# Attention and routed-expert kernel: when VectorE copies the transposed probabilities out of PSUM, and five smaller moves

## The chip, the cores and the metric

One core of a Trainium2 chip runs the whole program. The metric is the device time of one execution in microseconds (us), lower is better. Five engines work side by side, each through its own list of instructions in order: PE (TensorE; its weight loads are shown apart as PEld), DVE (VectorE), ACT (ScalarE), POOL (GpSimd) and SP (SyncE, which here issues DMAs). They meet only at semaphores.

## The reference

Sixteen batches of 512 rows with 128 features. For each batch, with `xn` the layer norm of `x`:

```
q, k, v = xn @ Wq + bq, xn @ Wk + bk, xn @ Wv + bv      # 16 heads of 64
att  = softmax(causal(q k^T / 8)) / 8
attn = concat_heads(att v) @ proj
gate = softmax(l2norm(xn Wp^T + bp) @ l2norm(sim) * exp(min(temp, c)))
ffn  = xn W^T + gate_top1 * (xn Wd_e^T) Wu_e^T          # the one expert of four with the largest gate
out  = x + attn + ffn
```

All is float32. The kernel splits float32 operands into a high and a low part ("hi", "lo") and adds three products.

## The kernel before, in words

A batch is 32 **units**, one a step `s`: a pair of heads (8 pairs) times a block of 128 query rows (4 blocks). Unit `s` is block `s % 4` of pair `s // 4`, and has 128 * (s % 4 + 1) key columns, since later keys are masked. In step `s` each engine does its own part of several units, in an order written out by hand in its function `step`:

- PE: `score` writes the scores of unit s, head 0 then head 1 (L1226, L1229 for s % 4 = 0; else L1247 and L1250 for each head). Then `transpose` turns the probabilities of unit s-3, both heads, into `ptp[0]` and `ptp[1]` (L1259). Then a job, if step s has one: k for the next pair (L1130) at s % 4 = 0, v (L1135) at 2, 6, 10, 14, 18, 22, 29, 30, q (L1130) at s % 4 = 3. At s % 4 = 1 come the 32 value matmuls of a pair (L1283), in some steps parts of the output projection (L1295), at 24 the base layer (L1304, L1309).
- DVE: `maximum` (L939) reads the scores of unit s out of PSUM, head 0 then head 1, adds the mask, and writes the row minimum of the negated scores through an accumulator read; `router` does its pieces of the expert choice; `reciprocals` (L927) inverts the sums of unit s-1; `evacuate_pt` (L951) copies head 1 of the turned unit s-3 out of `ptp[1]`; `low_z` (L957) makes the low half of a pair's z; then the low halves of k and q (L825, L829) and the statistics of the layer norm.
- ACT: exponentials of unit s (L688), head 0 of the turned unit s-3 (L699), high halves, v.
- POOL: probabilities times reciprocals (L603), low half of k (L567), a few router and norm operations.

There is one PSUM bank of scores for each head. So PE waits on `sm_ready`, which each maximum raises, before it writes a bank again. For s % 4 = 0 both heads lie in bank 0. Before scores of the steps after it the wait is:

```
wait(pe, sm_ready, c.head(s - 1, 1 if i == 1 else h))      # i = s % 4, for i > 0
```

that is, for unit 4p+1 both maxima of unit 4p must be done before head 0; for units 4p+2 and 4p+3 head h waits for the maximum of head h of the unit before. In turn `evacuate_pt` waits on `t_ready`, which PE raises after the last transpose of head 1, later in the same step than both heads' scores.

Ahead of the first batch PE turns the weights and makes the first q and k. `LATER` are three jobs of the first batch that lie outside the loop: v 0, v 1 (steps 29, 30) and q 1 (step 31). SP loads everything; `projs` (512 KB) is the last of the loads, and k_twice is then filled by small DMAs from k_hi.

Of the kernel before, what the change touches and what calls it, by code (L numbers as in the profile page):

```python
# [40 lines left out]
P = 128  # L41
# [32 lines left out]
LAG_Z = 10  # L74
# [137 lines left out]
def build(nc, x, Wq, bq, Wk, bk, Wv, bv, proj, W, Wp, bp, sim, temp, Wd, Wu, out):  # L212
    with ExitStack() as ctx:
# [187 lines left out]
        def _(sp):  # L401
# [23 lines left out]
            sp.dma_start(projs, proj.rearrange("(c p) e -> p c e", p=P)).then_inc(proj_loaded, 16)  # L425

# [70 lines left out]
        def _(pool):  # L497
# [80 lines left out]
            for h in range(2):  # L578
# [4 lines left out]
            nc.gpsimd.tensor_tensor(gated_t[:], token_heads[:, 0:S], token_heads[:, S:2 * S], ALU.add)\  # L583
                .then_inc(heads_marked, 1)
            pool.wait_ge(heads_marked, 4)
            pool.wait_ge(proj_loaded, 16)
            nc.gpsimd.tensor_copy(proj_hi[:], projs).then_inc(proj_split, 1)
            pool.wait_ge(proj_split, 1)
            nc.gpsimd.tensor_tensor(proj_lo[:], projs, proj_hi[:].bitcast(F32), ALU.subtract).then_inc(proj_split, 1)

            def sim_root():
                pool.wait_ge(simsq_ready, 1)
                nc.gpsimd.tensor_tensor(sim_norm[:, 1, :], sim_norm[:, 0, :], power[:, 1, 0:NEXP], ALU.pow)\
                    .then_inc(simnorm_ready, 1)
                pool.wait_ge(simnorm_ready, 1)

# [8 lines left out]
            def batch(b, last):  # L605
                c = Counts(pool, b)
                for s in range(UNITS):
# [19 lines left out]
                    if b == 0 and s == 0:  # L627
                        sim_root()
                    if s in JOBS and JOBS[s][0] == "k" and not (last and s in AHEAD):
                        pad_low_keys(c, s)  # L630
                    if s == STEP_RSTD and not last:
# [13 lines left out]
        def _(act):  # L645
# [79 lines left out]
            weights(4)  # L725

# [26 lines left out]
            def batch(b, first, last):  # L753
                c = Counts(act, b)
                for s in range(UNITS):
                    step(c, s, first, last)
                    if first and s == 0:
                        for js in LATER:
                            job(setup, js)
                        weights(5)  # L760
                    if first and s == 1:
                        gate_factor()
# [23 lines left out]
        def _(dve):  # L786
# [100 lines left out]
            def similarities():  # L887
                dve.wait_ge(sim_loaded, 32)
                nc.vector.tensor_scalar(temp_c[:], temp_b[:], CLAMP_MAX, None, ALU.min).then_inc(temp_ready, 1)
                link(nc.vector.tensor_tensor(sim_sq[:], sim_b[:], sim_b[:], ALU.mult))  # L890
                nc.vector.tensor_reduce(sim_norm[:, 0, :], sim_sq[:].rearrange("p a b -> p b a"), AX_X, ALU.add)\
                    .then_inc(simsq_ready, 1)
# [36 lines left out]
            def maximum(c, s):  # L929
                cols = width(s)  # L930
                for h in range(2):
                    bank, first_col = place(s, h)
                    scored, turned = c.fixed(c.head(s, 1 if s % NBLK == 0 else h)), c.fixed(c.head(s - NROT, h))

                    dve.wait_ge(consts_ready, 3)
                    dve.wait_ge(s_ready, scored)

                    wait(dve, t_ready, turned)
                    nc.vector.tensor_tensor_reduce(  # L939
                        out=prob[:, s % NROT, h, 0:cols], in0=scores[bank][:, first_col:first_col + cols], in1=mask[:, S - cols:S],  # L940
                        scale=-INV_SCALE, scalar=HUGE, op0=ALU.add, op1=ALU.min,
                        accum_out=nmax[:, s % NROT, h:h + 1]).then_inc(sm_ready, 1)
# [23 lines left out]
            def router(c, t):  # L966


                def prior(n):
                    dve.wait_ge(r_chain, c.at(R_CHAIN, n))  # L970

                def over_experts(m):
                    return m.unsqueeze(2).to_broadcast([P, NBLK, NEXP])

                t -= R_FIRST
                logits, shifted, exps, weights, chosen, ranked, first, routed = (lg[:, n, :, :] for n in range(1, 9))
                if t == 0:
# [4 lines left out]
                if t == 6:  # L982

                    dve.wait_ge(unorm_root, c.at(1, 1))
                    prior(1)
                    nc.vector.tensor_tensor(logits, lg[:, 0, :, :], over_experts(unorm[:, 2, :]), ALU.mult)\
                        .then_inc(r_chain, 1)
                if t == 6:
                    prior(2)
                    nc.vector.tensor_reduce(row[:, 0, :], logits, AX_X, ALU.max).then_inc(r_chain, 1)  # L990
                if t == 7:
                    prior(3)
                    nc.vector.tensor_tensor(shifted, logits, over_experts(row[:, 0, :]), ALU.subtract)\
                        .then_inc(lg_ready, 1)
                if t == 13:
# [3 lines left out]
                if t == 13:  # L999
                    prior(4)  # L1000
                    nc.vector.reciprocal(row[:, 2, :], row[:, 1, :]).then_inc(r_chain, 1)
                if t == 14:
                    prior(5)
                    nc.vector.tensor_tensor(weights, exps, over_experts(row[:, 2, :]), ALU.mult).then_inc(r_chain, 1)
                if t == 14:
                    prior(6)
                    nc.vector.tensor_reduce(row[:, 3, :], weights, AX_X, ALU.max).then_inc(r_chain, 1)
                if t == 15:
                    prior(7)
                    nc.vector.tensor_tensor(chosen, weights, over_experts(row[:, 3, :]), ALU.is_ge)\  # L1010
                        .then_inc(r_chain, 1)
                if t == 15:
                    prior(8)
# [410 lines left out]
```

## Time and profile before

| | us |
|---|---|
| three runs | 1374.68, 1376.75, 1377.0; median 1376.75 |
| the profiled execution, its own time | 1376.77 |
| its span, first to last instruction | 1375.0 |
| PE busy | 1350.0 (98%) |
| DVE busy | 1106.6 (80%) |
| ACT busy | 1077.1 (78%) |
| POOL busy | 971.9 (71%) |

The span is the program as the profile shows it; the 1.8 us between span and time lie around it. A matmul's row shows its start and how long it is under way; matmuls overlap, so what one costs is the distance from its start to the next one's start. The same holds for VectorE, whose rows overlap their successors by some 0.1 us.

### The profile page before, as it was taken

The numbers are of one execution on the slowest core, as the hardware profiler recorded it, in microseconds if no ns is written. First come the engines' busy times: TensorE is split into PE (matmuls) and PEld (weight loads), VectorE is DVE, ScalarE is ACT, GpSimd is POOL, SyncE is SP. The second block draws the span as 40 slices with busy tenths as digits, with TensorE's granted clock in tenths as the row PEclk, the third lists the DMA queues.
The fourth block names the chain that finished last, engine by engine and source line by source line (L and its number), as shares of the span: only waits on it lengthen the run. The fifth ranks groups of instructions, "written<-read, shape, count | busy, mean of one in ns | idle before, by whom it ended". The sixth has DMA issues, their size and how long they took to land.

```text
span 1375.0 us, 34724 instructions
## 1 busy us (share of the span) xinstructions
PE 1350.0 (98%) x10925; PEld 1140.4 (83%) x10925; DVE 1106.6 (80%) x4015; ACT 1077.1 (78%) x3161; POOL 971.9 (71%) x1421
## 2 busy tenths in 40 slices
PE   6999999999999999999999999999999999999998
PEld 4788888888888888888888888888888888888886
DVE  6877878788787887879788787887878878787784
ACT  4787877878777787787778878777887887878784
POOL 5777766777767777767777677776676776677664
PEclk9999999999999999999999999999999999999999
DMA  5444444444445445444544544444454444445441
GB/s 128 108 112 105 116 120 97 116 110 115 108 105 131 98 104 125 112 109 103 117 112 105 123 103 110 112 116 113 95 121 118 101 116 113 119 94 118 114 101 47
DMA packets 112690, 150.87 MB, mean 110 GB/s; under 512 B 18239, under 2 KB 47230, under 8 KB 112510
## 3 DMA queue, kind: packets, MB, share of 16 engines
q1 hardware_dynamic: 111646, 148.36, 45.6%
q8 instruction: 91, 1.49, 0.5%
q14 instruction: 89, 0.73, 0.2%
q10 hardware_dynamic: 864, 0.29, 0.1%
HBM read 10.69 MB, written 4.19 MB: 11 GB/s over the span
## 4 chain that ended last, share of the span: by engine, by line
PE 90%; DVE 5%; issue 1%; SPq 0%; DMA 0%; ACT 0%; DVEq 0%
PE zp L1283 22%; PE ptp L1259 20%; PE jobp L1130 12%; PE scores L1247 11%; PE scores L1250 9%; PE outp L1295 6%; PE jobp L1135 5%; DVE prob L939 2%; PE scores L1229 1%; DVE pt L951 1%; PE scores L1226 1%; PE jobp L1145 1%; PE outp L1304 1%; DVE z_lo L957 1%; PE jobp L1150 1%
## 5 line engine op out<-in xcount | busy, mean ns | idle before, releaser
L603 POOL TENSOR_TENSOR prob<-prob,rden 128x128 f32<-128x128 f32 (+3 forms) x1024 | 713.4, 724 | 347.2 <-DVE rden L927 345.1
L939 DVE CUSTOM_DVE_ANT_0 prob<-scores,mask 128x128 f32<-128x128 f32 (+3 forms) x1024 | 461.8, 488 | 220.8 <-issue 203.4
L688 ACT ACTIVATE prob<-prob,nmax 128x128 f32<-128x128 f32 (+3 forms) x1024 | 567.1, 559 | 38.9 <-DVE nmax L939 38.8
L1259 PE MATMUL ptp<-ident,prob 128*128 128x128 f32 x2560 | 375.7, 275 | 6.4 <-DVE pt L951 5.6
L1259 PEld LDWEIGHTS ptp<-ident,prob 128*128 128x128 f32 x2560 | 293.4, 141 | 44.8 <-issue 16.0
L1283 PE MATMUL zp<-pt,v_sb 128*64 128x64 f32 (+3 forms) x4096 | 307.7, 303 | 0.2 <-ACT pt L699 0.2
L699 ACT ACTIVATE pt<-ptp 128x128 f32<-128x128 f32 (+3 forms) x512 | 220.6, 431 | 108.2 <-PE ptp L1259 106.5
L1247 PE MATMUL scores<-k_twice,q_parts 128*128 128x256 f32 (+2 forms) x768 | 268.2, 357 | 0.3 <-DVE nmax L939 0.3
L1283 PEld LDWEIGHTS zp<-pt,v_sb 128*64 128x64 f32 x4096 | 221.3, 137 | 51.7 <-issue 19.5
L1250 PE MATMUL scores<-k_low,q_parts 128*128 128x256 f32 (+2 forms) x768 | 253.7, 338 | 0.0
L951 DVE COPY pt<-ptp 128x128 f32<-128x128 f32 (+3 forms) x512 | 243.2, 475 | 2.1 <-PE ptp L1259 1.3
L688 ACT ACTIVATION_READ_ACCUMULATOR prob<-prob,nmax 128x1 f32 x1024 | 199.9, 195 | 0.0
L1247 PEld LDWEIGHTS scores<-k_twice,q_parts 128*128 128x128 f32 x768 | 144.0, 188 | 62.9 <-issue 42.7
L567 POOL CAST k_low<-k_lo 64x512 fp32r<-64x512 f32 x256 | 156.9, 613 | 35.0 <-DVE k_lo L825 21.2
L677 ACT ACTIVATE z_hi<-zp 128x512 fp32r<-128x512 f32 x128 | 76.7, 599 | 131.8 <-PE zp L1283 131.8
L1250 PEld LDWEIGHTS scores<-k_low,q_parts 128*128 128x128 f32 x768 | 144.7, 188 | 15.2
L829 DVE SCALAR_TENSOR_TENSOR q_lo<-jobp,bqk,q_hi 128x512 fp32r<-128x512 f32 x128 | 95.6, 747 | 7.2 <-ACT q_hi L669 2.0
L825 DVE SCALAR_TENSOR_TENSOR k_lo<-jobp,bqk,k_hi 128x512 fp32r<-128x512 f32 x128 | 95.1, 743 | 1.8 <-ACT k_hi L666 1.7
L957 DVE TENSOR_TENSOR z_lo<-zp,z_hi 128x512 fp32r<-128x512 f32 x128 | 87.1, 680 | 2.4 <-ACT z_hi L677 2.4
L666 ACT ACTIVATE k_hi<-jobp,bqk 128x512 fp32r<-128x512 f32 x128 | 87.0, 680 | 0.2 <-PE jobp L1194 0.2
L669 ACT ACTIVATE q_hi<-jobp,bqk 128x512 fp32r<-128x512 f32 x128 | 86.1, 672 | 0.8 <-PE jobp L1184 0.7
L939 DVE DVE_READ_ACCUMULATOR2_ANT nmax<- 128x1 f32 x1024 | 85.1, 83 | 0.2
(183 smaller groups left out, 1841.7 us busy)
## 6 DMA issues: line engine op xcount, KB each, us to landing
k_twice<-k_hi SPq DMA_DIRECT2D x508, 128.0 KB, 2.3
q_parts<-q_lo SPq DMA_DIRECT2D x256, 128.0 KB, 2.4
q_parts<-q_hi SPq DMA_DIRECT2D x254, 128.0 KB, 2.3
xin<-in_L_attn_x_dram SPq DMA_DIRECT2D x16, 256.0 KB, 3.7
xres<-in_L_attn_x_dram SPq DMA_DIRECT2D x16, 256.0 KB, 3.1
out_dram<-osb SPq DMA_DIRECT2D x15, 256.0 KB, 2.6
pt<-in_L_attn_Wq_dram SPq DMA_DIRECT2D x1, 512.0 KB, 4.5
pt<-in_L_attn_Wk_dram SPq DMA_DIRECT2D x1, 512.0 KB, 6.2
```

The lines of the kernel that those rows point to most:

```text
L567: nc.gpsimd.tensor_copy(k_low[own(h), h, n % 2, :], k_lo[own(h), :].bitcast(F32))\
L603: nc.gpsimd.tensor_tensor(part, part, scale, ALU.mult).then_inc(pn_ready, 1)
L688: nc.scalar.activation(part, part, ACT.Exp, bias=nmax[:, s % NROT, h:h + 1], scale=-1.0, accum_out=den[:, s % NROT, h:h + 1]).then_inc(p_r ...
L699: nc.scalar.activation(pt[:, p % 2, 0, 0:i + 1, P * i:P * i + P], src, ACT.Copy)\
L939: nc.vector.tensor_tensor_reduce(out=prob[:, s % NROT, h, 0:cols], in0=scores[bank][:, first_col:first_col + cols], in1=mask[:, S - cols:S ...
L951: nc.vector.tensor_copy(pt[:, p % 2, 1, 0:i + 1, P * i:P * i + P], src).then_inc(pt_ready[1], 1)
L957: nc.vector.tensor_tensor(low, both, high.bitcast(F32), ALU.subtract).then_inc(z_ready, 1)
L1130: done = nc.tensor.matmul(dst[:], a[w][:, cols], m[:], start=a is w_hi and m is high, stop=a is w_lo)
L1247: nc.tensor.matmul(scores[h][:, 0:width(s)], q_parts[:, h, p % 2, queries], k_twice[:, h, p % 2, 0:width(s)], start=True, stop=False)
L1250: nc.tensor.matmul(scores[h][:, 0:width(s)], q_parts[:, h, p % 2, queries], k_low[:, h, p % 2, 0:width(s)], start=False, stop=True).then_i ...
L1259: done = nc.tensor.transpose(ptp[h][:, P * j:P * j + P], prob[:, s % NROT, h, P * j:P * j + P], ident[:])
L1283: done = nc.tensor.matmul(zp[DH * odd:DH * odd + DH, z0 + P // 2 * j:z0 + S // 2], v_sb[:, j, col:col + DH], seen, start=j == NBLK - 1, st ...
```

## The change

1. In DVE's `step`, `maximum` is called for one head at a time, and `reciprocals` and `evacuate_pt` stand between the two. 2. `low_z` follows a step later (11 steps behind instead of 10). 3. The router chain moves: its parts stand in steps 5, 6, 7, 9, 10 and 13 instead of 6 to 15, in groups of two to six operations; the aggregates of the norm move from step 13 to 17. 4. PE makes v 0 and v 1 ahead of the first scores and only q 1 after them; ACT evacuates them there. 5. SP issues the load of `projs` after the first q and k moves have landed; POOL splits `projs` after its second unit instead of ahead of the first. 6. In the first steps of batch 0 two weight parts, the similarities and the up-weights change places on DVE, ACT and POOL.

The core of the diff:

```diff
-LAG_Z = 10
+LAG_Z, LAG_LOW_Z = 10, 11
...
-STEPS_STATS, STEP_AGGR, STEP_VAR = (5, 9), 13, 17
+STEPS_STATS, STEP_AGGR, STEP_VAR = (5, 9), 17, 17
...
-STEP_PRODUCTS, STEP_UNORM, STEP_EXPERTS = 3, 6, 11
+STEP_PRODUCTS, STEP_UNORM, STEP_EXPERTS = 3, 4, 7
 R_CHAIN = 14
-R_FIRST = 12
+STEP_SUMS, STEP_LOGITS, STEP_WEIGHTS, STEP_FIRST, STEP_PARTS = 5, 6, 9, 10, 13
...
-            sp.dma_start(projs, proj.rearrange("(c p) e -> p c e", p=P)).then_inc(proj_loaded, 16)
...
+            sp.wait_ge(qk_moved[0], setup.moved(NPAIR))
+            sp.dma_start(projs, proj.rearrange("(c p) e -> p c e", p=P)).then_inc(proj_loaded, 16)
...
             def step(c, s, first=False, last=False, tail=False):
-                if not tail:
-                    maximum(c, s)
-                    router(c, 2 * s)
-                unit = due(s, 1, 1, first, tail)
-                if unit is not None:
-                    reciprocals(c, unit)
-                unit = due(s, LAG_T, 1, first, tail)
-                if unit is not None:
-                    evacuate_pt(c, unit)
-                p = due(s, LAG_Z, NBLK, first, tail)
+                def follow():
+                    unit = due(s, 1, 1, first, tail)
+                    if unit is not None:
+                        reciprocals(c, unit)
+                    unit = due(s, LAG_T, 1, first, tail)
+                    if unit is not None:
+                        evacuate_pt(c, unit)
+
+                maximum(c, s, 0)
+                follow()
+                maximum(c, s, 1)
+                router_early(c, s)
+                p = due(s, LAG_LOW_Z, NBLK, first, tail)
                 if p is not None:
                     low_z(c, p)
                 if s == STEP_FINAL and not first:
                     final(c)
-                if tail:
-                    return
+                router_late(c, s)
...
@@ PE, ahead of the first step, and in it
+            pe.wait_ge(w_lo_ready, 3)
+            for s in LATER[:2]:
+                job(setup, s)
             pe.wait_ge(small_ready, 3)
...
                 if first and s == 0:
-                    later()
+                    job(setup, LATER[2])
```

`router_early` holds the groups of steps 5, 6 and 10, `router_late` those of 9 and 13; the operations are those of `router`. On POOL the split of `projs` (L587, L589) moves into `projection_parts`, called after step 1 of batch 0.

In steady state the lists of PE, ACT and SP are the same as before. On DVE, the end of a step with s % 4 = 2 and the start of the next, in batch 0 (L939 is the maximum, L951 the copy of the turned unit, L927 the reciprocal, L957 z's low half; in the changed file L943, L955, L932, L961). Before:

```order
L939 ISA prob,nmax<-scores,mask 128x384
L939 ISA nmax 128x1
L939 ISA prob,nmax<-scores,mask 128x384
L939 ISA nmax 128x1
L927 RECIPROCAL rden<-den 128x2
L951 COPY pt<-ptp 128x4x128
L957 TENSOR_TENSOR z_lo<-zp,z_hi 128x8x64
```

and in the changed kernel:

```order
L943 ISA prob,nmax<-scores,mask 128x384
L943 ISA nmax 128x1
L932 RECIPROCAL rden<-den 128x2
L955 COPY pt<-ptp 128x4x128
L943 ISA prob,nmax<-scores,mask 128x384
L943 ISA nmax 128x1
```

The copy of four blocks now stands ahead of the second maximum, and z's low half is gone from this step. The step with s % 4 = 0, before:

```order
L939 ISA prob,nmax<-scores,mask 128x128
L939 ISA nmax 128x1
L939 ISA prob,nmax<-scores,mask 128x128
L939 ISA nmax 128x1
L927 RECIPROCAL rden<-den 128x2
L951 COPY pt<-ptp 128x2x128
L829 SCALAR_TENSOR_TENSOR q_lo<-jobp,bqk,q_hi 128x512
```

and in the changed kernel:

```order
L943 ISA prob,nmax<-scores,mask 128x128
L943 ISA nmax 128x1
L932 RECIPROCAL rden<-den 128x2
L955 COPY pt<-ptp 128x2x128
L943 ISA prob,nmax<-scores,mask 128x128
L943 ISA nmax 128x1
L835 SCALAR_TENSOR_TENSOR q_lo<-jobp,bqk,q_hi 128x512
```

Here too the copy (two blocks) stands ahead of the second maximum. On PE, from the last weight part to q 1 ahead of and in the first step; before (L1226 and L1229 are the first scores, L1135 is v, L1130 q):

```order
L1163 MATMUL ptp<-ident,pt 128x128 x8
L1226 MATMUL scores<-k_low,q_hi 128x256
L1229 MATMUL scores<-k_twice,q_parts 128x128 x2
L1135 MATMUL jobp<-w_hi,xt_hi 128x512
L1135 MATMUL jobp<-w_lo,xt_hi 128x512
L1135 MATMUL jobp<-w_hi,xt_lo 128x512
L1135 MATMUL jobp<-w_hi,xt_hi 128x512
L1135 MATMUL jobp<-w_lo,xt_hi 128x512
L1135 MATMUL jobp<-w_hi,xt_lo 128x512
L1130 MATMUL jobp<-xq_hi,w_hi 128x512
```

and in the changed kernel (L1218 and L1221 the scores, L1129 v, L1124 q):

```order
L1157 MATMUL ptp<-ident,pt 128x128 x8
L1129 MATMUL jobp<-w_hi,xt_hi 128x512
L1129 MATMUL jobp<-w_lo,xt_hi 128x512
L1129 MATMUL jobp<-w_hi,xt_lo 128x512
L1129 MATMUL jobp<-w_hi,xt_hi 128x512
L1129 MATMUL jobp<-w_lo,xt_hi 128x512
L1129 MATMUL jobp<-w_hi,xt_lo 128x512
L1218 MATMUL scores<-k_low,q_hi 128x256
L1221 MATMUL scores<-k_twice,q_parts 128x128 x2
L1124 MATMUL jobp<-xq_hi,w_hi 128x512
```

The six matmuls of v 0 and v 1 now stand ahead of the first scores.

## Rows read from the trace of the kernel before

**Rows 1.** The page, part 1: busy time of each engine, share, instructions.
```profile
PE 1350.0 (98%) x10925; PEld 1140.4 (83%) x10925; DVE 1106.6 (80%) x4015; ACT 1077.1 (78%) x3161; POOL 971.9 (71%) x1421
```

**Rows 2.** Waits of PE: who, until whom; us in all, times, longest.
```profile
PE ptp L1259 <- DVE pt L951: 5.6, 17, 0.8
PE scores L1247 <- DVE nmax L939: 0.3, 1, 0.3
```

**Rows 3.** Timeline of PE, steps 2 and 3 of batch 7: start, us, what.
```profile
613.56 1.03 PE L1259 MATMUL ptp<-ident,prob 128*128 128x128 f32 x8
...
615.59 0.39 PE L1247 MATMUL scores<-k_twice,q_parts 128*128 128x512 f32 x1
```

**Rows 4.** Timeline of DVE over the same stretch.
```profile
613.50 0.56 DVE L939 CUSTOM_DVE_ANT_0 prob<-scores,mask 128x384 f32<-128x384 f32 x1 [2.16 <-issue]
...
613.98 0.55 DVE L939 CUSTOM_DVE_ANT_0 prob<-scores,mask 128x384 f32<-128x384 f32 x1
...
614.63 0.69 DVE L951 COPY pt<-ptp 128x512 f32<-128x512 f32 x1
615.24 0.68 DVE L957 TENSOR_TENSOR z_lo<-zp,z_hi 128x512 fp32r<-128x512 f32 x1
```

**Rows 5.** Timeline of PE in batch 0, a score matmul that waited for DVE.
```profile
34.90 0.38 PE L1247 MATMUL scores<-k_twice,q_parts 128*128 128x256 f32 x1 [0.27 <-DVE nmax L939]
35.12 0.28 PE L1250 MATMUL scores<-k_low,q_parts 128*128 128x256 f32 x1
```

**Rows 6.** Timeline of DVE, the accumulator read which that matmul waited for.
```profile
34.76 0.08 DVE L939 DVE_READ_ACCUMULATOR2_ANT nmax<- 128x1 f32 x1
```

**Rows 7.** Timeline of PE, steps 4 and 5 of batch 7.
```profile
617.97 0.62 PE L1259 MATMUL ptp<-ident,prob 128*128 128x128 f32 x4
...
618.90 0.39 PE L1130 MATMUL jobp<-xt_hi,w_lo 128*128 128x512 f32 x1
619.13 0.28 PE L1247 MATMUL scores<-k_twice,q_parts 128*128 128x256 f32 x1
619.24 0.28 PE L1250 MATMUL scores<-k_low,q_parts 128*128 128x256 f32 x1
```

**Rows 8.** Timeline of PEld, the weight load of the matmul at 619.13.
```profile
618.90 0.19 PEld L1247 LDWEIGHTS scores<-k_twice,q_parts 128*128 128x128 f32 x1
```

**Rows 9.** Timeline of DVE over the same stretch.
```profile
618.27 0.29 DVE L939 CUSTOM_DVE_ANT_0 prob<-scores,mask 128x128 f32<-128x128 f32 x1 [0.81 <-issue]
...
618.49 0.29 DVE L939 CUSTOM_DVE_ANT_0 prob<-scores,mask 128x128 f32<-128x128 f32 x1
...
618.78 0.41 DVE L951 COPY pt<-ptp 128x256 f32<-128x256 f32 x1
619.10 0.74 DVE L829 SCALAR_TENSOR_TENSOR q_lo<-jobp,bqk,q_hi 128x512 fp32r<-128x512 f32 x1
```

**Rows 10.** Timeline of PE, steps 26 and 27 of batch 7.
```profile
676.28 1.03 PE L1259 MATMUL ptp<-ident,prob 128*128 128x128 f32 x8
...
677.67 0.41 PE L1247 MATMUL scores<-k_twice,q_parts 128*128 128x512 f32 x1
```

**Rows 11.** Timeline of DVE, step 8 of batch 7: end of a maximum, next reciprocal.
```profile
628.64 0.08 DVE L939 DVE_READ_ACCUMULATOR2_ANT nmax<- 128x1 f32 x1
628.73 0.17 DVE L927 RECIPROCAL rden<-den 128x2 f32<-128x2 f32 x1
```

**Rows 12.** Timeline of PE, the first score matmul of the program.
```profile
19.00 0.55 PE L1226 MATMUL scores<-k_low,q_hi 128*128 128x256 f32 x1 [4.53 <-DMA k_twice<-k_hi]
```

**Rows 13.** Timeline of DVE, low half of the third weight part, before it.
```profile
15.37 0.69 DVE L869 TENSOR_TENSOR w_lo<-zp,w_hi 128x512 fp32r<-128x512 f32 x1 [0.43 <-ACT w_hi L649]
```

**Rows 14.** Windows: busy by engine, then PE's granted clock, DMA share, GB/s.
```profile
19.00:22.30 3.30, 3.30 (x9) 2.73 (x10) 2.24 (x9) 1.48 (x5) 2.38 (x1) 0.50 0.00 0
...
26.70:28.30 1.60, 0.30 (x2) 0.00 (x0) 0.76 (x2) 1.60 (x6) 0.99 (x2) 1.00 0.66 166
28.30:31.90 3.60, 3.56 (x24) 3.21 (x25) 3.46 (x13) 2.06 (x8) 2.46 (x4) 1.00 0.73 195
```

More of the change, by code:

```diff
@@ L595, in sim_root, with projection_parts @@
                 pool.wait_ge(simnorm_ready, 1)
+            sim_root()
+            nc.gpsimd.tensor_tensor(gated_t[:], token_heads[:, 0:S], token_heads[:, S:2 * S], ALU.add)\
+                .then_inc(heads_marked, 1)
+            pool.wait_ge(heads_marked, 4)
+            def projection_parts():
+                pool.wait_ge(proj_loaded, 16)
+                nc.gpsimd.tensor_copy(proj_hi[:], projs).then_inc(proj_split, 1)
+                pool.wait_ge(proj_split, 1)
+                nc.gpsimd.tensor_tensor(proj_lo[:], projs, proj_hi[:].bitcast(F32), ALU.subtract)\
+                    .then_inc(proj_split, 1)
             def normalise(c, s):
@@ L725, in _ @@
             weights(4)
+            for js in LATER[:2]:
+                job(setup, js)
             def gate_factor():
@@ L757, in batch @@
                     if first and s == 0:
-                        for js in LATER:
-                            job(setup, js)
+                        job(setup, LATER[2])
+                        gate_factor()
+                    if first and s == 1:
                         weights(5)
-                    if first and s == 1:
-                        gate_factor()
             batch(0, True, False)
@@ L927, in reciprocals, with maximum @@
                 nc.vector.reciprocal(rden[:, s % NROT, :], den[:, s % NROT, :]).then_inc(r_ready, 1)
-            def maximum(c, s):
+            def maximum(c, s, h):
                 cols = width(s)
[L931 to L942, printed above, removed]
+                bank, first_col = place(s, h)
+                scored, turned = c.fixed(c.head(s, 1 if s % NBLK == 0 else h)), c.fixed(c.head(s - NROT, h))
+                dve.wait_ge(consts_ready, 3)
+                dve.wait_ge(s_ready, scored)
+                wait(dve, t_ready, turned)
+                nc.vector.tensor_tensor_reduce(
+                    out=prob[:, s % NROT, h, 0:cols], in0=scores[bank][:, first_col:first_col + cols],
+                    in1=mask[:, S - cols:S], scale=-INV_SCALE, scalar=HUGE, op0=ALU.add, op1=ALU.min,
+                    accum_out=nmax[:, s % NROT, h:h + 1]).then_inc(sm_ready, 1)
             def evacuate_pt(c, s):
@@ L964, in final, with over_experts, router_early @@
                                         xres[:].rearrange("p n e -> p (n e)"), ALU.add).then_inc(final_ready, 1)
[L966 to L977, printed above, removed]
+            def over_experts(m):
+                return m.unsqueeze(2).to_broadcast([P, NBLK, NEXP])
+            logits, shifted, exps, shares, chosen, ranked, top, routed = (lg[:, n, :, :] for n in range(1, 9))
+            def router_early(c, s):
+                if s == STEP_SUMS:
                     dve.wait_ge(products_ready, c.at(1, 1))
@@ L1005, in router @@
[L1005 to L1010, printed above, removed]
+                    dve.wait_ge(r_chain, c.at(R_CHAIN, 5))
+                    nc.vector.tensor_tensor(shares, exps, over_experts(row[:, 2, :]), ALU.mult).then_inc(r_chain, 1)
@@ L1068, in step @@
                     variances(c)
-                router(c, 2 * s + 1)
             def batch(b, first, last):
@@ L1076, in batch @@
                         weights(3)
+                        job(before, LATER[2])
+                    if first and s == 1:
                         weights(4)
-                        similarities()
-                        for js in LATER:
-                            job(before, js)
                         experts_up()
-                    if first and s == 1:
                         weights(5)
@@ L1203, in _ @@
             weights(4)
+            pe.wait_ge(w_lo_ready, 3)
+            for s in LATER[:2]:
+                job(setup, s)
             pe.wait_ge(small_ready, 3)
-            def later():
-                pe.wait_ge(w_lo_ready, 3)
-                for s in LATER:
-                    job(setup, s)
             def value_bias():
@@ L1326, in step @@
                 if first and s == 0:
-                    later()
+                    job(setup, LATER[2])
                 unit = due(s, LAG_T, 1, first, tail)
```

75 lines of the change are left out of this document (30 added, 45 removed).

## The prediction

> **What bounds the kernel now.** I read the page first, then the waits of PE, then the timelines of PE and DVE side by side through one pair of heads in the middle of the run. PE is busy 98% of the span, the next engine, DVE, 80% [rows 1]. PE's waits for DVE are small: 5.6 us in 17 waits for the copy L951, about one a batch, and 0.3 us for a maximum [rows 2]. So PE runs its list almost without a hole, and the time is the length of that list. After the first steps the change leaves PE's list as it is; it can only take holes out of it or put holes into it. What it moves is DVE, and DVE's idle time (2.16 us ahead of one maximum, 0.81 us ahead of another [rows 4, 9]) says that DVE has time to spare on average. The question is whether DVE is late at the moments when PE asks.
>
> PE asks twice in a pair, and closely: ahead of head 1 of unit 4p+3 it needs the second maximum of unit 4p+2, and ahead of head 0 of unit 4p+1 the second maximum of unit 4p. Before, the second maximum followed the first at once. Now the copy L951 stands between, and the copy waits for PE's own transposes of the same step. This makes a closed loop inside a step: PE's last transpose, DVE's copy, DVE's second maximum, PE's next scores. Its length does not depend on how idle DVE is otherwise.
>
> **The loop from step 4p+2 to 4p+3.** PE's eight transposes start at 613.56 and end at 613.56 + 1.03 = 614.59; head 1 of the next scores starts at 615.59 [rows 3]. PE gives DVE 1.00 us. DVE needs: 0.04 until the copy starts (614.63, just behind the transposes; its first maximum was done long before), 0.61 for the copy of four blocks (614.63 to 615.24), 0.48 for the maximum of 384 columns (613.50 to 613.98) [rows 4], 0.08 for its accumulator read, which ends at 34.84, and 0.06 until PE goes on at 34.90 [rows 5, 6]. Sum 1.27, so PE starts 0.27 late. There is a second part. A matmul that had to wait starts with its weight load, and the next one comes 0.22 behind it (34.90 to 35.12) [rows 5]; where nothing waits the distance is 0.11 (619.13 to 619.24) [rows 7]. That adds 0.11. Hole: **0.38 us**, at 7 of the 8 pairs of a batch.
>
> A rule bears on the 0.11. The load of the matmul at 619.13 starts at 618.90, together with the matmul ahead of it [rows 7, 8], so a load in time costs nothing. The Trainium skill says (TensorE: Matmul & The Clock Gate, section Measured speedup vs the span model) that weight loads overlap running matmuls only where they use other row groups; both of these use all 128 rows, so by it no load would be hidden now, a late one would add nothing, and the sum below would be 26 us less. The trace does not agree with it.
>
> **The loop at step 26** has no v job between the transposes and the next scores: 676.28 + 1.03 = 677.31, and head 1 starts at 677.67 [rows 10], 0.36 after. DVE's 1.27 leaves 0.91, with the load 1.02 us, once a batch.
>
> **The loop from step 4p to 4p+1.** The four transposes end at 617.97 + 0.62 = 618.59, PE's next scores start at 619.13 [rows 7]: 0.54. DVE: 0.04, 0.32 for the copy of two blocks (618.78 to 619.10), 0.22 for the maximum of 128 columns (618.27 to 618.49) [rows 9], then 0.08 and 0.06 as above, 0.72. Late by 0.18, with the load **0.29 us**. It falls on 7 pairs; in step 24 four wide matmuls (base and experts) lie between and cover it.
>
> The other two transitions cost nothing: between 4p+1 and 4p+2 PE has 32 value matmuls, and head 0 of unit 4p+4 needs only the first maximum of 4p+3.
>
> A batch: 7 x 0.38 + 7 x 0.29 + 1.02 = 5.71 us, 16 batches: **+91.4 us**. What is queued behind the waiting copy on DVE (second maximum, low halves of k and q, z) comes later by about half a microsecond and is taken up by DVE's idle time of 0.81 and 2.16 us in the same pair [rows 4, 9]. ACT's exponential of head 1 waits with it; ACT, busy 78% of the span [rows 1], has the idle time for that. But the reciprocal, which needs that exponential, now also stands ahead of the second maximum. Where it waited in the trace it was 0.09 us (628.64 to 628.73) [rows 11]. I take nothing for it, and 0.09 at each of the 15 places as the upper end (+22 us).
>
> **What goes away.** The router's chain leaves the steps in which PE waited for L951, and the copy comes ahead of the second maximum: the 17 waits of 5.6 us [rows 2] go, with their 17 late loads of 0.11: **-7.5 us**. The router's operations themselves are the same and are put at nothing: the largest group stands in step 9, ahead of the idle 2.16 us; without that cover they would delay the first maximum of step 10, which PE needs only before step 11.
>
> **z's low half a step later** is put at nothing. It moves into the step ahead of the 0.81 us idle [rows 9], and PE overwrites z only two steps on. Without that cover it would push the next first maximum and with it the loop at 4p.
>
> **The start.** PE stood idle 4.53 us until k_twice had landed, and started the first scores at 19.00 [rows 12]; so it was free at 14.47. The 512 KB of `projs` were issued just ahead of the transfers that it waited for. Now `projs` comes after them, and PE has v 0 and v 1 to do, which need the low half that DVE ends at 15.37 + 0.69 = 16.06 [rows 13]. The hole shrinks to 1.59: **-2.9 us**. The ends are nothing (POOL now splits `projs` between two units, where PE or DVE may wait for it) and -4.5 (the whole hole). The exchanges of small operations in steps 0 to 3 lie within these ends.
>
> Sum against the profiled execution, 1376.8 us by its own time, which is also the median of the runs: 1376.8 + 91.4 - 7.5 - 2.9 = **1457.8 us**, 5.9% slower.
>
> **The rivals.**
> - *The loop is shorter than PE's own way.* If copy and maximum overlapped or PE's 1.00 and 0.54 us were longer, no hole would open; it decides at 0.27 and 0.18 us. Then only the savings are left: 1376.8 - 7.5 - 2.9 = 1366.4, faster. For it: DVE has 20% to spare. Against it: the distances are the same in every pair that I looked at, and DVE goes in order. 8%.
> - *Only the longer loop holds* (the one at 4p is hidden because copy and maximum are short): without 16 x 7 x 0.29 = 32.5 us, 1425. For it: it is late by 0.18 only. Against: the terms are measured to hundredths. 5%.
> - *The late load is free*, the page's rule above: without 16 x 15 x 0.11 = 26.4, 1431. Against it: the two distances [rows 5, 7]. 5%.
> - *The clock falls.* After the idle 4.53 us PE ran 3.3 us at a granted clock of 0.50, the lower of its two levels (1.2 and 2.4 GHz), but through a hole of 1.3 us (0.30 busy in 1.60) and after it at 1.00 [rows 12, 14]. If the 1.0 us hole of step 26 made it fall for as long, a batch would lose 3.3 / 2 = 1.65 more, 16 times 26: 1484. The Trainium skill (the same page, section A second HAM failure mode: psum-queue depth-cycling) tells of a kernel whose short idle times between groups of matmuls made the clock swing. No stretch after the start shows that here. 5%.
> - *The change does not do what it says*: the order of DVE's list shows that it does; no chance of its own.
>
> **How the numbers follow.** Chances: forecast 77%, the rivals 8, 5, 5 and 5%. A measurement can tell about 0.2% from no change. Faster is the first rival, 8%; within 0.2% would need holes that just cancel the savings, 1%; slower the rest, 91%. The range: downwards, the late loads free (-26.4) and the hole at step 26 half as long (-8), 1423; upwards, every reciprocal late by 0.09 (+22) and nothing saved at the start (+3), 1482. It takes in the second and third rival and leaves out the first and the clock.
>
> **What would show it.** In the profile after: waits of PE for DVE's nmax ahead of the score matmuls, some 15 a batch, 240 in all, of 0.2 to 1.0 us; PE's busy share near 93%; idle DVE just ahead of the copies of four blocks; no wait of PE for L951; the first scores by 18.8 or earlier; the clock at 1.00 throughout. It is wrong if those waits are few, if they sit in front of other matmuls, or if a batch is not near 89 us instead of 83.8.

## The result and the profile after

The changed kernel takes **1445.86 us** (median of 5 runs, 1445.18 to 1446.13) against 1377.0 us before: ratio 1.0503, 95% interval 1.0487 to 1.0518. It is 69 us slower; the prediction was 1457.8 us, range 1423 to 1482. Its profiled execution has a span of 1443.7 us and a granted clock of 1.000.

The page of the changed kernel, part 1, and groups of part 5 (busy us, mean ns | idle just before, what ended most of it):

```profile
PE 1399.1 (97%) x10925; PEld 1124.3 (78%) x10925; DVE 1144.1 (79%) x4015; ACT 1103.3 (76%) x3161; POOL 969.7 (67%) x1421
...
L943 DVE CUSTOM_DVE_ANT_0 prob<-scores,mask 128x128 f32<-128x128 f32 (+3 forms) x1024 | 495.7, 485 | 155.1 <-issue 136.1
L1251 PE MATMUL ptp<-ident,prob 128*128 128x128 f32 x2560 | 365.9, 274 | 0.0
L955 DVE COPY pt<-ptp 128x128 f32<-128x128 f32 (+3 forms) x512 | 250.2, 489 | 98.9 <-PE ptp L1251 89.4
```

VectorE now stands idle 98.9 us ahead of the copies, waiting for PE's transposes; the transposes no longer wait for the copy (5.6 us before, [rows 2]). PE, which bounds the kernel, still reads 97% busy [rows 1 had 98%], although its list became 5% longer. The waits, of all engines, show where the time is:

```profile
PEld scores L1239 <- DVE nmax L943: 138.2, 256, 2.4
...
DVE pt L955 <- PE ptp L1251: 89.4, 236, 1.3
...
PE scores L1239 <- DVE nmax L943: 14.4, 29, 2.0
```

Under PE itself there are 29 waits of 14.4 us; the other ones stand under PEld, the weight load, which is the instruction that waits. The load's engine has idle time anyway, so 138.2 us is no cost, and PE's row understates it, since the modelled end of one matmul lies over most of a short hole. What a hole costs has to be read from starts. Here is the loop from step 4p+2 to 4p+3 in batch 7, the stretch of [rows 3, 4], PE first:

```profile
641.21 1.04 PE L1251 MATMUL ptp<-ident,prob 128*128 128x128 f32 x8
...
643.50 0.50 PE L1239 MATMUL scores<-k_twice,q_parts 128*128 128x512 f32 x1
643.83 0.40 PE L1242 MATMUL scores<-k_low,q_parts 128*128 128x512 f32 x1
```

and VectorE:

```profile
641.15 0.56 DVE L943 CUSTOM_DVE_ANT_0 prob<-scores,mask 128x384 f32<-128x384 f32 x1 [1.86 <-issue]
...
642.28 0.69 DVE L955 COPY pt<-ptp 128x512 f32<-128x512 f32 x1 [0.48 <-PE ptp L1251]
642.89 0.55 DVE L943 CUSTOM_DVE_ANT_0 prob<-scores,mask 128x384 f32<-128x384 f32 x1
643.36 0.08 DVE L943 DVE_READ_ACCUMULATOR2_ANT nmax<- 128x1 f32 x1
```

The transposes end at 642.25. The copy starts 0.03 later, the second maximum 0.61 after that, its read ends at 643.44, and PE goes on at 643.50: 1.25 us after the transposes, where it took 1.00 before [rows 3]. This is the loop of the prediction link by link.

To price every place, the starts of PE's matmuls in two kernels were set side by side, position by position in a batch (PE's list is the same in all these kernels after the first batch), and the differences averaged over 11 batches. "Excess" below means that. From router matmul to router matmul a batch takes 88.27 us (median), against 83.75 before.

### The profile page after: what moved, and what is told of

Its sections match the earlier page's. It is cut to its first block and busy times, and to the rows that moved or that the text cites. A ratio compares the mean times of both kernels' runs of the same rounds, so it can differ in the third digit from the quotient of the medians.

```text
span 1443.7 us, 34725 instructions
## 1 busy us (share of the span) xinstructions
PE 1399.1 (97%) x10925; PEld 1124.3 (78%) x10925; DVE 1144.1 (79%) x4015; ACT 1103.3 (76%) x3161; POOL 969.7 (67%) x1421
## 5 line engine op out<-in xcount | busy, mean ns | idle before, releaser
L943 DVE CUSTOM_DVE_ANT_0 prob<-scores,mask 128x128 f32<-128x128 f32 (+3 forms) x1024 | 495.7, 485 | 155.1 <-issue 136.1
L1251 PE MATMUL ptp<-ident,prob 128*128 128x128 f32 x2560 | 365.9, 274 | 0.0
L955 DVE COPY pt<-ptp 128x128 f32<-128x128 f32 (+3 forms) x512 | 250.2, 489 | 98.9 <-PE ptp L1251 89.4
L1239 PE MATMUL scores<-k_twice,q_parts 128*128 128x256 f32 (+2 forms) x768 | 292.1, 388 | 30.7 <-DVE nmax L943 14.4
L1239 PEld LDWEIGHTS scores<-k_twice,q_parts 128*128 128x128 f32 x768 | 143.9, 187 | 185.9 <-DVE nmax L943 138.2
L961 DVE TENSOR_TENSOR z_lo<-zp,z_hi 128x512 fp32r<-128x512 f32 x128 | 87.6, 685 | 2.5 <-ACT z_hi L682 2.5
L932 DVE RECIPROCAL rden<-den 128x2 f32<-128x2 f32 x512 | 83.0, 162 | 5.4 <-ACT prob L693 3.7
```

Source lines behind the costliest of these rows:

```text
L943: nc.vector.tensor_tensor_reduce(out=prob[:, s % NROT, h, 0:cols], in0=scores[bank][:, first_col:first_col + cols], in1=mask[:, S - cols:S ...
L955: nc.vector.tensor_copy(pt[:, p % 2, 1, 0:i + 1, P * i:P * i + P], src).then_inc(pt_ready[1], 1)
L1239: nc.tensor.matmul(scores[h][:, 0:width(s)], q_parts[:, h, p % 2, queries], k_twice[:, h, p % 2, 0:width(s)], start=True, stop=False)
L1251: done = nc.tensor.transpose(ptp[h][:, P * j:P * j + P], prob[:, s % NROT, h, P * j:P * j + P], ident[:])
```

## The experiments

The runs of the kernel before that stood beside these have medians of 1375.5 to 1376.4 us. All kernels are edits of the changed one, but for the second and the ninth, which start from the kernel before.

### 1. Copy behind both maxima again

```diff
                 maximum(c, s, 0)
-                follow()
                 maximum(c, s, 1)
+                follow()
```

> The changed kernel with one thing undone: both maxima first, then reciprocals and copy, as before; z's low half, the router's steps and the start stay changed. Theory (the copy ahead of the second maximum makes the holes): the holes of about 5.6 us a batch go, 16 x 5.6 = 90 us, and what is left is the start, -3.7 us, and up to -1.0 us a batch; 1357 to 1373 us, so faster than before; PE's waits for nmax nearly none. Rival 1 (z's low half or the router's groups make DVE late): stays at 1430 to 1446 us. Rival 2 (the copy and the moves each do harm only together): also far under 1446, told apart by the next run.

**1359.28 us, ratio to the kernel before 0.9876 (0.9861 to 0.9891): faster than both.** One edit of two lines takes away 86.6 us. A batch takes 82.88 us. The excess of the changed kernel over this one is 5.39 us a batch (x16 = 86.2) and stands in the places named by the prediction and hardly anywhere else:

| place | of each, predicted | excess: late + late load |
|---|---|---|
| 4p+2 to 4p+3, 7 a batch | 0.27 + 0.11 | 0.26 + 0.105 |
| 4p to 4p+1, 7 a batch | 0.18 + 0.11 | 0.20 + 0.10 |
| step 26 to 27, once | 0.91 + 0.11 | 0.34 ahead of head 0, 0.57 + 0.09 at head 1 |
| transposes at two later places | nothing | -0.10, -0.08 |

### 2. The copy between, and nothing else of the change

In the kernel before, reciprocals and copy stand between the maxima; router, z's low half and the start are those of before.

```diff
-                    maximum(c, s)
-                    router(c, 2 * s)
+                maximum(c, s, 0)
...
                     evacuate_pt(c, unit)
+                maximum(c, s, 1)
+                router(c, 2 * s)
```

> The kernel before with one thing changed: reciprocals and copy between the two maxima; router, z's low half and the start as before. Theory: 1377 + 16 x (5.6 - 0.47) = 1459 us, 1445 to 1470, with PE's waits for nmax in the same three places of a pair (scores of units 4p+1 head 0, 4p+3 head 1, and 4p+3 of the seventh pair about 1.0 us). Rival 2 (harm only together with the other moves): under 1400 us.

**1470.51 us** (ratio 1.0687, 1.0669 to 1.0704), just over the upper end. The copy alone makes the loss, but with the router and z's low half in their old places it costs 94.2 us instead of 86.6. Two of the holes at 4p are wider: 0.79 us ahead of unit 9 and 1.04 us ahead of unit 17, against 0.20 elsewhere. VectorE ahead of the second one:

```profile
690.35 0.34 DVE L1032 CAST gated_parts<-gated 128x256 fp32r<-128x256 f32 x1
690.73 0.80 DVE L1036 TENSOR_TENSOR gated_parts<-gated,gated_parts 128x128 fp32r<-128x128 f32 x1
691.45 0.28 DVE L938 CUSTOM_DVE_ANT_0 prob<-scores,mask 128x128 f32<-128x128 f32 x1
...
691.73 0.40 DVE L950 COPY pt<-ptp 128x256 f32<-128x256 f32 x1
692.05 0.27 DVE L938 CUSTOM_DVE_ANT_0 prob<-scores,mask 128x128 f32<-128x128 f32 x1
```

Two router operations of step 15 push the first maximum of step 16 to 691.45, and the whole chain of the step with it. With the router in its new steps no such hole stands anywhere. Ahead of unit 9 it is the reciprocal that is late (VectorE, ScalarE, VectorE, PE):

```profile
665.25 0.68 DVE L980 TENSOR_REDUCE lg<-uprod 128x16 f32<-128x512 f32 x1
```

```profile
667.17 0.73 ACT L688 ACTIVATE prob<-prob,nmax 128x512 f32<-128x512 f32 x1 [0.63 <-DVE nmax L938]
```

```profile
668.88 0.17 DVE L927 RECIPROCAL rden<-den 128x2 f32<-128x2 f32 x1 [0.60 <-ACT prob L688]
```

```profile
669.63 0.39 PE L1246 MATMUL scores<-k_twice,q_parts 128*128 128x256 f32 x1 [0.63 <-DVE nmax L938]
```

Router sums and z's low half at the end of step 6 push the maxima of unit 7, ScalarE waits 0.63 us for the first of them, and the reciprocal of unit 7, which stands between the maxima of step 8, waits 0.60 us for them, with the copy and the second maximum behind it. It does so in each of the 11 batches, and in the changed kernel in none. No run took this alone.

### 3 and 4. One loop at a time

The steps are 1, 2, 3 in the first kernel and 0, 1, 3 in the second.

```diff
+                between = s % NBLK in (1, 2, 3)
                 maximum(c, s, 0)
-                follow()
+                if between:
+                    follow()
                 maximum(c, s, 1)
+                if not between:
+                    follow()
```

> The changed kernel with copy and reciprocals between the maxima only in steps with s % 4 = 1, 2, 3; in steps with s % 4 = 0 they stand behind both maxima. Theory: only the loop from 4p+2 to 4p+3 is left, 7 x (0.263 + 0.104) + 1.015 = 3.58 us a batch: 57 us over the kernel with the copy behind both maxima everywhere, about 1415 to 1430. If the two loops share their cost (DVE late from one into the other), more than 57.

> The changed kernel with copy and reciprocals between the maxima only in steps with s % 4 = 0, 1, 3. Theory: only the loop from 4p to 4p+1 is left, 7 x (0.19 + 0.10) = 2.03 us a batch: 32 us over the kernel with the copy behind both maxima everywhere, about 1390 to 1405. The rival of the prediction that only the longer loop holds: no more than 5 us over it. The excess of this run and of the one with s % 4 = 1, 2, 3, added, should give the whole distance between the changed kernel and the one with the copy behind both maxima, to within 5 us.

**1412.09 us and 1396.74 us**, 52.8 and 37.5 over experiment 1. The sum is 90.3, the whole distance 86.6: within the 5 us. Each kernel has the seven holes of its own loop at the same size as in the changed kernel and none of the other's. So the two loops hold independently, and the rival with the longer loop alone is out: without what the odd steps cost (4.5 us, the next experiment) the 4p loop comes to 32.9 us, 32.5 predicted. One thing does not fit the prediction: 0.34 us ahead of head 0 of unit 27 stand in both kernels, and so does the gain of 0.10 at the transposes of step 24. Counted twice in the sum, they are 16 x 0.24 = 3.8 us of it, which is about its distance from 86.6.

### 5. Copy between in steps 4p+1 and 4p+3 only

```diff
+                between = s % NBLK in (1, 3)
```

> The changed kernel with copy and reciprocals between the maxima only in steps with s % 4 = 1 and 3. Theory of the prediction: these transitions cost nothing, 1359 us. But in the run with s % 4 = 0, 1 and 3 a hole of 0.34 us was left ahead of head 0 of unit 27: if the copy of step 25 makes it, it stands here too, 16 x 0.34 = 5.4 us, 1365; if the copy of step 24 does, 1359.

**1363.81 us**, 4.5 over experiment 1. The 0.33 us ahead of unit 27 are here too, so the copy in an odd step makes them. The chain goes through ScalarE, as the trace of the changed kernel shows behind step 25:

```profile
704.18 0.51 ACT L693 ACTIVATE prob<-prob,nmax 128x256 f32<-128x256 f32 x1 [0.28 <-DVE nmax L943]
...
704.69 0.58 ACT L667 ACTIVATE xt<-jobp 128x512 f32<-128x512 f32 x1
705.16 0.59 ACT L668 ACTIVATE xq_hi<-jobp 128x512 fp32r<-128x512 f32 x1
```

and VectorE after that, PE last:

```profile
705.85 0.91 DVE L823 TENSOR_TENSOR xq_lo<-xt,xq_hi 128x512 fp32r<-128x512 f32 x1 [1.04 <-ACT xq_hi L668]
706.68 0.68 DVE L839 TENSOR_TENSOR xt_lo<-xt,xt_hi 128x512 fp32r<-128x512 f32 x1
707.28 0.55 DVE L943 CUSTOM_DVE_ANT_0 prob<-scores,mask 128x384 f32<-128x384 f32 x1
...
707.76 0.15 DVE L932 RECIPROCAL rden<-den 128x2 f32<-128x2 f32 x1
707.84 0.67 DVE L955 COPY pt<-ptp 128x512 f32<-128x512 f32 x1
708.42 0.54 DVE L943 CUSTOM_DVE_ANT_0 prob<-scores,mask 128x384 f32<-128x384 f32 x1
```

```profile
706.71 1.04 PE L1251 MATMUL ptp<-ident,prob 128*128 128x128 f32 x8
707.89 0.50 PE L1239 MATMUL scores<-k_twice,q_parts 128*128 128x512 f32 x1
...
709.03 0.50 PE L1239 MATMUL scores<-k_twice,q_parts 128*128 128x512 f32 x1 [0.40 <-DVE nmax L943]
```

The late second maximum of unit 25 delays ScalarE's exponential of head 1, behind it the three evacuations of the turned norm (L667 to L669), and these VectorE's two halves (L823, L839), which stand ahead of the first maximum of unit 26. PE waits for both heads of unit 27.

### 6. Only the reciprocals between

```diff
                 maximum(c, s, 0)
+                inverse()
                 maximum(c, s, 1)
+                copy()
```

> The changed kernel with only the reciprocals between the maxima and the copy behind both. Theory (the copy's wait for the same step's transposes makes the holes): as with both behind, 1359 us, 1355 to 1364, hole by hole. Rival (the reciprocal, which waits for ACT's exponential of head 1, holds the second maximum back): 0.09 us at 15 places a batch, up to 22 us more, 1381.

**1359.11 us**, the same as experiment 1. With the router in its new steps the reciprocal's price is nil.

### 7. Other work between the maxima

```diff
                 maximum(c, s, 0)
+                p = due(s, LAG_Z, NBLK, first, tail)
+                if p is not None:
+                    low_z(c, p)
                 maximum(c, s, 1)
```

with reciprocals and copy behind both maxima.

> The changed kernel with z's low half between the two maxima of the steps with s % 4 = 2 (10 steps behind, as in the kernel before), reciprocals and copy behind both maxima. So VectorE does a comparable piece of work between the maxima, but one that waits for nothing of this step's PE. Theory: no closed loop, no holes, 1359 us, 1355 to 1366. Rival (any work between the maxima makes PE late): a hole of the order of 0.2 to 0.4 us in 7 pairs and more at step 26, 25 to 60 us more, 1385 to 1420.

**1374.35 us**, between the two expectations. VectorE in step 4p+2 of batch 7:

```profile
610.94 0.56 DVE L943 CUSTOM_DVE_ANT_0 prob<-scores,mask 128x384 f32<-128x384 f32 x1 [2.16 <-issue]
...
611.42 0.69 DVE L961 TENSOR_TENSOR z_lo<-zp,z_hi 128x512 fp32r<-128x512 f32 x1
612.03 0.55 DVE L943 CUSTOM_DVE_ANT_0 prob<-scores,mask 128x384 f32<-128x384 f32 x1
```

From the start of what stands between to the second maximum it takes 0.61 us here as with the copy (642.28 to 642.89), but nothing waits: the maximum starts at 612.03, just as the transposes end (611.00 + 1.03), and the seven holes are gone. What is left is 0.50 + 0.09 us at step 26, where no v job gives PE anything to do, and 0.27 us at the transposes of steps 8 and 9. So in the seven pairs it is the wait for the same step's transposes that costs; at step 26 0.6 us of work that waits for nothing costs 0.50 us all the same. I had not expected the latter.

### 8. The heads of the copies exchanged

```diff
-                dve.wait_ge(t_ready, c.head(s, 1))
+                dve.wait_ge(t_ready, c.head(s, 0))
...
-                src = ptp[1][:, 0:width(s)].rearrange("p (j q) -> p j q", q=P)
+                src = ptp[0][:, 0:width(s)].rearrange("p (j q) -> p j q", q=P)
```

and the reverse on ScalarE.

> The changed kernel with the heads of the copies exchanged: VectorE copies head 0 of the turned unit, ScalarE head 1. Reciprocals and copy stay between the maxima; but head 0's transposes end about 0.5 us (4 of 8) or 0.3 us (2 of 4) ahead of head 1's, so VectorE is released earlier by that. Theory: the holes at 4p+2 (late by 0.27) and 4p (late by 0.18) go; at step 26 0.91 - 0.5 and the late load, some 0.5 us, is left: 1359 + 16 x 0.5 = 1367, 1357 to 1385. Rival (what counts is the work between the maxima, not its wait): holes as in the changed kernel, 1430 to 1446. ScalarE's copy comes later by as much and may hold back the next transposes; that would show as waits of PE for ACT's pt.

**1400.42 us**: half right. The seven holes at 4p+2 are gone, by the earlier release alone. Those at 4p shrink only from 0.20 to 0.15 + 0.10 at five of seven places and to 0.10 + 0.11 ahead of unit 29; ahead of unit 9 the hole grows to 0.39 + 0.10, which was not followed. Step 26 keeps 0.07 + 0.57 + 0.09. VectorE at 4p in this kernel, where the transposes end at 626.96:

```profile
626.63 0.29 DVE L943 CUSTOM_DVE_ANT_0 prob<-scores,mask 128x128 f32<-128x128 f32 x1 [0.22 <-issue]
...
626.88 0.17 DVE L932 RECIPROCAL rden<-den 128x2 f32<-128x2 f32 x1
626.96 0.40 DVE L955 COPY pt<-ptp 128x256 f32<-128x256 f32 x1
627.28 0.28 DVE L943 CUSTOM_DVE_ANT_0 prob<-scores,mask 128x128 f32<-128x128 f32 x1
```

The copy could start when head 0's transposes are done, but VectorE reaches it only now: first maximum, read and reciprocal take until 626.96. At 4p two chains end within 0.1 us of each other, the wait for the transposes and VectorE's own, and taking one away leaves the other.

### 9 and 10. Where the gain of experiment 1 comes from

The start alone (parts 4 to 6 of the change), in the kernel before; PE's share of it:

```diff
+            pe.wait_ge(w_lo_ready, 3)
+            for s in LATER[:2]:
+                job(setup, s)
...
-                    later()
+                    job(setup, LATER[2])
```

Then experiment 1 with z's low half 10 steps behind:

```diff
-LAG_Z, LAG_LOW_Z = 10, 11
+LAG_Z, LAG_LOW_Z = 10, 10
```

> The kernel before with only the start changed (the values made ahead of the first scores, the load of projs after the first q and k moves, the small exchanges in the first steps); VectorE's order, router and z's low half as before. By the traces the first router matmul comes 3.7 us earlier in the changed kernel (24.74 to 21.04): 1376 - 3.7 = 1372.3 us, 1371 to 1374, and the batches after the first as before. The prediction's term is -2.9 with ends 0 and -4.5. Rival: the split of projs on POOL or the late loads give it back in the first batch, no change.

> The changed kernel with both maxima first and z's low half 10 steps behind again; only the router's steps and the start stay changed. The prediction puts the move of z's low half at nothing: then 1359 us, as with z's low half 11 steps behind, and the 0.86 us a batch that this kernel gains on the one before are the router's. Rival: three of the four gains (0.07 to 0.10 us each, 0.28 a batch) are those of z's low half: 1359 + 16 x 0.28 = 1363.5.

**1374.08 us** (ratio 0.9986, 0.9977 to 0.9995) and **1368.45 us** (0.9946, 0.9934 to 0.9959). The start gives 1.8 us by the medians. In the profiled executions the first router matmul comes 3.8 us earlier, but the first batch takes 0.6 us more and the later ones some 0.6 in all. In the first batch of the changed kernel, the likely reason:

```profile
26.57 1.10 POOL L597 CAST proj_hi<-pt 128x1024 fp32r<-128x1024 f32 x1
27.76 2.38 POOL L599 TENSOR_TENSOR proj_lo<-pt,proj_hi 128x1024 fp32r<-128x1024 f32 x1
...
30.18 0.29 DVE L923 CAST wut<-outp 96x128 fp32r<-96x128 f32 x1 [0.94 <-POOL proj_lo L599]
...
32.17 0.39 PE L1239 MATMUL scores<-k_twice,q_parts 128*128 128x256 f32 x1 [1.97 <-DVE nmax L943]
```

POOL's split of `projs` holds VectorE until 30.14, and PE then stands 1.97 us for a maximum. No run took this alone.

From the start alone to the second of these kernels it is 5.6 us, the router's and aggregates' part: the wait for L951 at step 16 is gone, 0.46 us a batch with its load. And z's low half one step later is worth **9.2 us** (1368.45 to 1359.28), more than the rival had said. With z's low half back, four places among the transposes (steps 8, 9, 13 and 29) lose 0.07 to 0.11 us each, 0.39 of 0.52 us a batch. The places of steps 9 and 29 are late in the kernel before too, those of 8 and 13 only with the router in its new steps: the split between router and z's low half is that of this order of the moves. VectorE from the end of step 6 into step 7:

```profile
620.38 0.68 DVE L961 TENSOR_TENSOR z_lo<-zp,z_hi 128x512 fp32r<-128x512 f32 x1
620.98 0.68 DVE L943 CUSTOM_DVE_ANT_0 prob<-scores,mask 128x512 f32<-128x512 f32 x1
...
621.58 0.68 DVE L943 CUSTOM_DVE_ANT_0 prob<-scores,mask 128x512 f32<-128x512 f32 x1
...
622.19 0.16 DVE L932 RECIPROCAL rden<-den 128x2 f32<-128x2 f32 x1
622.27 0.27 DVE L955 COPY pt<-ptp 128x128 f32<-128x128 f32 x1
```

and PE:

```profile
622.36 0.73 PE L1251 MATMUL ptp<-ident,prob 128*128 128x128 f32 x4
```

z's low half stands ahead of both maxima, so the copy ends at 622.54, after PE has begun the next transposes (622.36); the four take 0.73 us where they take 0.62 in experiment 1. At the transposes of step 9 it is POOL's normalisation that is late, behind the late reciprocal; the other two places were not followed.

### 11. The odd steps but step 25

```diff
+                between = s % NBLK in (1, 3) and s != STEP_BASE + 1
```

> The changed kernel with copy and reciprocals between the maxima only in steps with s % 4 = 1 and 3, but not in step 25. In the run with s % 4 = 1 and 3 the only hole was 0.33 us ahead of head 0 of unit 27, and one late weight load of 0.10 was gone. If step 25 makes that hole: 1359.2 - 16 x 0.10 = 1357.6 us, the fastest of the runs. If another odd step makes it, 1363 again.

**1359.15 us.** The hole ahead of unit 27 is gone, so step 25 was its source, and the gain of 0.10 us at the transposes of step 24 is kept; a batch takes 82.76 us, 0.12 less than in experiment 1. The first batch takes 1.8 us more (82.97 against 81.20; why is open), and the total is no better. Experiments 1, 6 and 11 are the best kernels here, and not told apart.

### 12. Only the copy between

```diff
                 maximum(c, s, 0)
-                follow()
+                unit = due(s, LAG_T, 1, first, tail)
+                if unit is not None:
+                    evacuate_pt(c, unit)
                 maximum(c, s, 1)
+                unit = due(s, 1, 1, first, tail)
+                if unit is not None:
+                    reciprocals(c, unit)
```

> The changed kernel with only the copy between the maxima and the reciprocals behind both. Theory: the copy's wait carries the holes; the reciprocal overlaps its neighbours and is 0.08 us of VectorE's way where nothing else waits (in steps with s % 4 = 0 and in step 26, where in the changed kernel the copy starts straight behind it), nothing where the copy waits for the transposes: 0 to 8 x 0.08 us a batch less, 1435 to 1446 us. Rival, the upper end of the prediction: each reciprocal 0.09 late at 15 places, 22 us less, 1424.

**1446.33 us**, the changed kernel's time; excess 5.44 us a batch over experiment 1, in the same places (ahead of unit 27 0.52 + 0.51 instead of 0.34 + 0.57). The copy alone carries the loss.

## Why the prediction was right

- **The two loops** held, in mechanism and size: seven times 0.37 (0.38 predicted) and seven times 0.30 (0.29). Together with step 26 and the two gains of 0.10 and 0.08 the copy's place costs 86.6 us by experiment 1, 91.4 predicted. For 4p+2 the reason was the given one (experiments 7 and 8). For 4p it was half of it: VectorE's own chain of maximum, reciprocal and copy ends as late as the transposes.
- **Step 26**: 1.00 us, 1.02 predicted. Head 1 starts 1.28 us after the transposes (707.75 to 709.03), the predicted 1.27, but there is a second way to it: 0.34 us of the hole stand ahead of head 0 and come from step 25. "The other two transitions cost nothing" failed there, and so did "has the idle time for that": the maximum of unit 25 delays ScalarE, and with it the first maximum of unit 26, which the prediction, going by the other pairs, took to be "done long before". No run has the copy between in step 26 and not in step 25, so what would be left without the 0.34 is open, and that the size came out so well is in part luck.
- **The late weight load** costs 0.09 to 0.11 us at every place, which makes up 1.5 us a batch. That it is the load is read from the trace and not tested: a load in time starts 0.22 ahead of its matmul (642.54, 642.76), a late one together with it (643.50). The rival that called it free would have 16 x 15 x 0.10 = 24 us less. The Trainium skill has the line behind that rival (TensorE: Matmul & The Clock Gate, section The mechanism; the prediction names the section that follows): weight loads overlap running matmuls only when they use other row groups. The trace does not agree with that line, since the load at 642.54 runs under matmuls that use all 128 rows, as it does. The same section also lets a load into the background weight buffer run ahead; no run here shows whether this is one.
- **The waits for L951**: -7.5 predicted, -5.6 measured with the router's new places (0.46 a batch saved, some of it lost by 0.06 and 0.11 at two transposes).
- **z's low half** was the term that failed: put at nothing, it is worth -9.2 us. I asked only whether it delays the next maximum, and did not see that the copy and the reciprocal behind it come late for PE's next transposes, by some 0.1 us at a time. PE's waits in the profile do not show that: with z's low half back they have one wait for the copy, 0.8 us in the whole run.
- **The start**: -2.9 predicted, -1.8 measured. The first scores start at 17.80 instead of 19.00, behind a hole of 1.29 us (1.59 predicted). The 4.53 us were those of one execution: in experiment 2, which has the start of the kernel before, the hole is 3.31 and the first scores start at 18.39. And the prediction did not count the stretch at a granted clock of 0.50, the lower level [rows 14]. The profiled execution of the changed kernel has none at the start (1.00 from 13 to 40 us), but it depends on the execution: five executions of the kernel before with a mean granted clock of 1.000 took 1375.1 us on average, four of the start alone 1374.2. So of the 1.8 us some 0.9 are left where no such stretch stands in either. Against the start stands the first batch.
- **The reciprocal**, the upper end of +22 us, is nothing in the changed kernel (experiments 6 and 12). With the router in its old steps it does hold the copy back, at one place of a batch (experiment 2, unit 9).
- **The clock** stayed at 1.000 with 256 waits of weight loads on record, and in none of the fourteen profiles did it fall between 39 us and the last 4: the rival of the falling clock is out.

The misses, measured less predicted: holes -4.8, z's low half -9.2, router +1.9, start +1.1, in sum -11.0 of the 11.9 us between forecast and result; the other 0.9 lie in the starting point (1376.8 in the forecast, 1375.9 beside experiment 9). The four terms are the steps of one way from the kernel before to the changed one (1375.9, 1374.1, 1368.5, 1359.3, 1445.9), so that they add up says nothing for any one of them. In another order they come out otherwise: with the other moves still to come the copy's place costs 94.2 us (experiment 2). Of the signs named ahead, one was wrong: PE's busy share is 97%, not 93%, for the reason given with the waits.

## What to carry to other kernels

When an instruction that waits for engine A is put ahead of one that A waits for, write down the closed loop with its times and compare it with A's own time between the two points; idle time of the other engine, here 20%, does not shorten it. Behind each moved instruction, price also the small lateness of what the bound engine reads next: 0.1 us at four places a batch was 6 of the 9 us that z's low half was worth. What stands inside the loop is free only as long as its own inputs come in time: the reciprocal cost nothing in the changed kernel and held the copy 0.60 us in experiment 2. And where an engine runs short overlapping instructions, price holes by distances between starts, not by idle time or busy share.

## What the runs showed of the hardware

The granted clock does not follow from one hole of PE alone (windows: start to end, length, busy PE, PEld, DVE, ACT, POOL, clock, DMA share, GB/s). In experiment 1 PE stood for 2.27 us up to 32.13, and the clock then fell to 0.50, the lower of its two levels:

```profile
33.50:36.50 3.00, 3.00 (x14) 2.77 (x13) 3.00 (x10) 1.64 (x6) 2.92 (x5) 0.50 0.66 154
```

In the changed kernel the hole of 1.97 us at the same place left it at 1.00:

```profile
34.00:37.00 3.00, 2.43 (x14) 1.83 (x15) 3.00 (x12) 1.61 (x6) 2.92 (x6) 1.00 0.69 159
```

But in experiment 3 (steps 4p+1 to 4p+3) it fell after a hole of 1.59 us, and in experiment 2 it stayed at 1.00 after one of 3.31 us:

```profile
34.00:36.00 2.00, 1.93 (x8) 1.70 (x8) 2.00 (x8) 0.60 (x2) 1.92 (x4) 0.50 0.91 209
```

```profile
20.00:23.00 3.00, 2.50 (x12) 1.66 (x10) 2.42 (x6) 1.95 (x5) 1.46 (x1) 1.00 0.00 0
```

Nor does it follow from the kernel: one and the same kernel has executions with a mean granted clock of 1.000 and others of 0.998 (the kernel before 12 and 13 of those beside the experiments), and of the twelve profiles with the new start eight have such a stretch between 31 and 39 us and four have none. What decides stays open. The price differs as well. Those 12 executions of the kernel before took 1375.0 us on average and those 13 took 1376.8. The first batch takes 81.20 us in experiment 1, with the stretch, and 81.03 in experiment 6, without it, where the later batches are the same (82.88 and 82.85).
